# Token attention: raw score products issued ahead of the bilinear ones by half of a unit's heads

## The reference

```python
def _L0_attn_ref(x, ...):                      # H = 16 heads of HD = 8, t = 256 tokens
    qkv = (x @ qkv_w.T).reshape(b, t, 3, H, HD)
    q, k, v = ...                              # each (b, H, t, HD)
    raw = einsum('bhid,bhjd->bhij', q, k)
    scores = sips_alpha * tanh(raw / sips_beta)
    soft_bits = tanh(x @ hex_w.T)              # 6 columns
    scores += lam * einsum('bid,bjd->bij', soft_bits, soft_bits)[:, None] / 2
    hexc = tanh(x @ q6_w.T)                    # 6 columns
    scores += einsum('bid,hde,bje->bhij', hexc, Mh, hexc) / 6 * (2 * sigmoid(scale_logit))
    attn = softmax(where(causal, scores, -inf))
    return (attn @ v) ... @ out_w.T
```

## Time and profile before

| | |
|---|---|
| median of 3 runs | 4148.58 us (4145.99 to 4149.01) |
| profiled execution, its own time | 4149.29 us |
| span of the profiled execution | 4147.5 us, so 1.8 us lie around it |
| token stage, from the start of the span | about 0 to 905 us |
| busy over the span: PE, DVE, ACT, POOL | 94%, 74%, 64%, 45% |
| products of L607 and of L613 | 2048 passes each (1024 of 256 columns, 1024 of 128) |

### The profile page before, as it was taken

The page is one execution under the profiler, slowest core; times in us unless marked ns, Lnnn a source line. Parts: engine busy times, 40 slices in busy tenths (PEclk is TensorE's granted clock), DMA queues, the critical chain, the costliest instruction groups (busy, mean ns, idle before and its releaser), DMA issues. The chain is left out here.

```text
span 4147.5 us, 105164 instructions
## 1 busy us (share of the span) xinstructions
PE 3897.3 (94%) x35227; PEld 3023.3 (73%) x35481; DVE 3050.4 (74%) x7206; ACT 2662.1 (64%) x6345; POOL 1866.7 (45%) x1769
## 2 busy tenths in 40 slices
PE   7999999979999989899999898999999999999999
PEld 6777777756677765577777656777777777789998
DVE  6888888878888875688888685555555565556666
ACT  6888888857777763477777436666666666633333
POOL 4555555547777751466656343333434333321111
PEclk9999999989999999999999999999999999999999
DMA  3000000000000001000000010000000000000000
GB/s 107 1 0 0 0 0 0 0 6 20 19 23 19 23 20 30 14 13 15 13 15 13 22 24 21 1 0 0 0 0 0 0 0 0 0 5 9 9 9 10
DMA packets 68908, 48.04 MB, mean 12 GB/s; under 512 B 38216, under 2 KB 57552, under 8 KB 68688
## 3 DMA queue, kind: packets, MB, share of 16 engines
q1 hardware_dynamic: 68816, 46.82, 4.4%
HBM read 13.01 MB, written 4.19 MB: 4 GB/s over the span
## 5 line engine op out<-in xcount | busy, mean ns | idle before, releaser
L1648 ACT ACTIVATE l_probs<-l_act,l_neg_max 128x128 f32<-128x128 f32 (+1 forms) x1024 | 416.2, 426 | 273.7 <-DVE l_neg_max L1605 271.1
L383 POOL TENSOR_TENSOR t_probs<-t_probs,t_neg_max 128x512 f32<-128x512 f32 x384 | 392.8, 1044 | 392.7 <-DVE t_neg_max L444 392.7
L1585 POOL TENSOR_TENSOR l_probs<-l_probs,l_sums 128x512 f32<-128x512 f32 x384 | 391.6, 1041 | 365.7 <-DVE l_sums L1613 365.7
L1605 DVE TENSOR_REDUCE l_neg_max<-l_act 128x2 f32<-128x512 f32 (+1 forms) x384 | 247.0, 685 | 356.6 <-PE l_act L1760 164.0
L1966 ACT ACTIVATE e_hT<-e_act 128x512 f32<-128x512 f32 x256 | 152.9, 597 | 285.4 <-PE e_act L1987 285.4
L437 DVE SCALAR_TENSOR_TENSOR t_probs<-t_tanh_qk,scalars_sb,t_dve 128x512 f32<-128x512 f32 x384 | 269.6, 744 | 88.4 <-ACT t_tanh_qk L541 39.9
L832 POOL TENSOR_TENSOR w_swappedQ<-w_rawQ,w_table 128x512 f32<-128x512 f32 x128 | 162.3, 1290 | 309.8 <-ACT w_rawQ L1049 309.8
L541 ACT ACTIVATE t_tanh_qk<-t_act,t_inv_beta 128x512 f32<-128x512 f32 x384 | 243.1, 684 | 89.3 <-PE t_act L607 89.0
L1999 PEld LDWEIGHTS e_dve<-e_sb,e_hT 128*128 128x128 f32 x2048 | 268.9, 192 | 13.3
L1085 ACT ACTIVATE w_probs<-w_a,w_bias,w_invQ 128x128 f32<-128x128 f32 x512 | 186.0, 469 | 143.5 <-DVE w_bias L952 143.5
L832 POOL TENSOR_TENSOR w_swappedK<-w_rawK,w_table 128x512 f32<-128x512 f32 x128 | 228.7, 1808 | 92.7 <-ACT w_rawK L1049 92.7
(11 more groups left out here) (259 smaller groups left out, 10672.8 us busy)
## 6 DMA issues: line engine op xcount, KB each, us to landing
w_v_mid<-w_v SPq DMA_DIRECT2D x128, 130.0 KB, 2.3
z<-w_z_copy SPq DMA_DIRECT2D x32, 128.0 KB, 2.0
h<-z SPq DMA_DIRECT2D x32, 128.0 KB
out<-x_sb SPq DMA_DIRECT2D x32, 128.0 KB, 1.8
h<-z SPq DMA_DIRECT2D x32, 127.0 KB
wqkv_sb<-L_ffn_wqkv SPq DMA_DIRECT2D x2, 768.0 KB, 5.9
kv_up_sb<-L_attn_w_kv_up SPq DMA_DIRECT2D x1, 1024.0 KB, 8.4
e_sb<-L_ffn_w SPq DMA_DIRECT2D x1, 1024.0 KB, 5.7
```

The source lines that it names most:

```text
L383: nc.gpsimd.tensor_tensor(p, p, neg_max[:, j, 0:len(gs)].unsqueeze(2) .broadcast_to((P, len(gs), P * (t + 1))), ALU.add).then_inc(shifted. ...
L1585: nc.gpsimd.tensor_tensor(p, p, sums[:, at, 0:len(hs)].unsqueeze(2) .broadcast_to((P, len(hs), P * (t + 1))), ALU.mult).then_inc(divided.s ...
L1605: nc.vector.tensor_reduce(neg_max[:, units.index(name), 0:len(hs)], to_act.bank("s" + name, back)[:, :].rearrange("p (h j) -> p h j", h=le ...
L1648: ins = nc.scalar.activation(probs[:, at % SLOTS, s * width:(s + 1) * width], bank[:, s * width:(s + 1) * width], ACT.Exp, bias=neg_max[:, ...
```

## The change

Only the order in which `scores` issues its products on TensorE changes. The waits for free banks stay ahead of them all; the mask products stay behind them all; operands, shapes, banks, flags and signals of each product stay as they are.

```diff
-                    for s, g in enumerate(gs):
-                        at, tile, last = slice(s * width, (s + 1) * width), slice(P * t, P * t + P), s == len(gs) - 1
+                    tile = slice(P * t, P * t + P)
+
+                    def raw(s, name):
+                        far = rows((unit(name)[0] + GROUPS // 2) % GROUPS)
+                        ins = nc.tensor.matmul(to_act.bank("raw" + name, back)[:, s * width:(s + 1) * width],
+                                               q[u][far, gs[s], tile], k[u][far, gs[s], 0:width],
+                                               start=s == 0, stop=s == len(gs) - 1)
+                        if s == len(gs) - 1:
+                            ins.then_inc(to_act.filled.sem, 1)
+
+                    def bil(s, name):
+                        near = rows(unit(name)[0])
+                        nc.tensor.matmul(to_dve.bank("bil" + name, back)[:, s * width:(s + 1) * width],
+                                         left[u][near, gs[s], tile], bits[u][near, 0:width],
+                                         start=s == 0, stop=False)
+
+                    behind_raw = len(gs) // 2
+                    for s in range(len(gs) + behind_raw):
                         for name in names:
-                            far = rows((unit(name)[0] + GROUPS // 2) % GROUPS)
-                            ins = nc.tensor.matmul(to_act.bank("raw" + name, back)[:, at], q[u][far, g, tile],
-                                                   k[u][far, g, 0:width], start=s == 0, stop=last)
-                            if last:
-                                ins.then_inc(to_act.filled.sem, 1)
-                        for name in names:
-                            near = rows(unit(name)[0])
-                            nc.tensor.matmul(to_dve.bank("bil" + name, back)[:, at], left[u][near, g, tile],
-                                             bits[u][near, 0:width], start=s == 0, stop=False)
+                            if s < len(gs):
+                                raw(s, name)
+                            if s >= behind_raw:
+                                bil(s - behind_raw, name)
```

## The result

The changed kernel takes 4153.5 us (median of 20 runs, 4147.5 to 4155.6) against 4147.1 us (20 runs, 4143.1 to 4149.9): a ratio of **1.0014**, 95% interval 1.0007 to 1.0020. The ratio gives 5.8 us more (2.9 to 8.3), the difference of the medians is 6.4 us. The profiled execution has 4152.8 us (span 4151.0) against 4149.3. In these two traces the start of the last block of scores lies 867.5 us behind that of the first after the change, 863.0 us before: all that the profiled execution lost, 3.5 us, is lost in the token stage.

A forecast was written before the change was run, and what follows sets the result against it. TensorE sets the token stage's pace (748.92 of 800 us busy), VectorE close behind. Later mask products cost 0 to 3.4 us, taken as 2: profiled 4149.3 + 2 = 4151.3, median 0.7 lower, so 4150.6 us, range 4145 to 4156.

The forecast's parts named there:

- the wait that it had named as cover: TensorE's idle time ahead of L607 on VectorE's probabilities copy and combine, 1.1 us per sequence, which could absorb the delay.
- the step that failed: Score blocks: each row group works through its own list from block start, so all passes keep their times; cost nothing.
- Rival 2: Score blocks: limited row-group room makes a and b stand idle; 4200 us, most of it 4163 to 4205, chance 0.27.
- its point: Row-group queue: the stall decides from where more than one product waits; 7 instructions in two-head, 11 in four-head blocks.
- its sign in the timeline: Block start: only L607 passes, L613 beginning 0.2 to 0.45 us later, and TensorE's waits on VectorE partly reduced.
- its case of two products' room: With room for two products per row group, only four-head blocks are hit, 0.22 us each: 14 us, 4163 us.
- Rival 1: Score blocks: raw banks finish earlier by program order, shortening TensorE's loop waits by 12 us; 4137 us, chance 0.09.
- The rule of the Trainium skill that I had weighed: TensorE: matmuls start and end strictly in program order, only weight loads pulled ahead; a block would take 1.94 us.

The follow-up runs named there:

- `left` on 128 rows: Kernel before with products left0 and left1 on 128 rows instead of 12 (zero rows added): -10.0 us, 0.9972; same edit on the changed kernel: +0.4 us, 0.9998.
- one head ahead: Kernel before with raw products running one head ahead of bilinear ones in both kinds of block: +2.1 us, ratio 1.0006.
- pairs: Kernel before with products issued in pairs of one row group (A0 A1 B0 B1 a0 a1 b0 b1) in both kinds of block: -1.5 us, ratio 0.9998.
- longer bilinear lists: Kernel before, old order, each four-head block doing its first bilinear products of each twin three times: +13.8 us, ratio 1.0033.
- All raw first: Kernel before with all raw products of a block issued ahead of all its bilinear ones: +38.3 us, ratio 1.0096.
- three of A first: Kernel before with four-head blocks only reordered to start A0 A1 A2 B0 a0 b0: +6.0 us, ratio 1.0015.
- filled wait: Kernel before with three overwritten 512-column products ahead of turn 4's wait for bilinear banks: -1.0 us, ratio 0.9997.
- the last run: Kernel before with turn 4's raw products issued after the raw-bank wait alone, bilinear ones after their own wait: -4.8 us, ratio 0.9988.

## Why the prediction was right, and where it was not

- **Forecast and bounds.** 4150.6 us, +2 us, in a range of 4145 to 4156; measured 4153.5 us, +5.8 us or 0.14%, inside that range and clear of zero. That it came out so near is luck: the forecast had missed a stall of 20.8 us in all, and most of that was taken away by the wait that it had named as cover and by the clock, for which it had no term.
- **Two-head blocks: right.** Four rounds, four row groups in step, mask 0.014 us later (expected 0.013), no time that can be measured in the run with these blocks alone.
- **Four-head blocks: the step that failed** is "If a row group starts on its list as soon as the block begins, then every pass starts where it does now": the row groups of a and b start 0.33 us late. I priced the four-head block at 0.027 us; it costs 0.325 us. Rival 2 named the mechanism ("a row group can hold only so much"), its point (7 instructions fit, 11 don't) and its sign in the timeline (L613 starting 0.2 to 0.45 us late); its case of two products' room holds. Its size was off: 0.22 us a block instead of 0.325, since A2 is taken in when A0's second pass is over (0.33 us), not when it starts (0.22 us).
- **The sum of that rival, with the measured size,** would have been 0.325 x 64 + 0.015 x 128 = 22.7 us, and too high. Two terms were missing from it. TensorE's wait ahead of turn 1 shrank: with no half-clock stretches about (`left` on 128 rows), the mean distance from turn 0 to turn 1 is 4.01 us without the change and 3.73 with it, 0.28 x 32 = 9 us, seen in the waits on the combine (10.4 and 3.4 us). That is the cover of 1.1 us per sequence that I had named, of which a quarter was used. And eight half-clock stretches fewer: the kernel before has 863.0 - 852.7 = 10.3 us more than with the edit of `left`, for ten stretches, so 1.0 us each, 8 us in all. 22.7 - 9 - 8 = 5.7 us; measured 5.8. The close agreement is luck too: between the two kernels with `left` on 128 rows the same account gives 22.7 - 9 = 13.7 us, and the medians are 10.4 us apart, the two traces' blocks 12.9; and in the changed kernel a step with a stretch is 1.6 us longer and the next no shorter, so that its two cost 3 us and not 2. The account holds to some 3 us.
- **Why fewer stretches.** Shown: they go when the `left` products use all rows, and come in one place of the step. The products on 12 rows are not enough for one: they stand in every step of every kernel without that edit, and most steps have no fall. That the changed kernel has two where the kernel before has ten goes with its undisturbed steps of 27.2 to 27.6 us against 26.8 to 27.2; one head ahead and pairs, in between, have six and five. The granted clock over the span, 0.986 to 0.989 in all 20 runs of the changed kernel and 0.982 to 0.986 in all runs of the kernel before beside the experiments, says the same as the two traces. Why a longer step meets fewer of them was not tested, and longer is not always better. The longer bilinear lists, at 27.5 to 27.7 us, had four. All raw first, with undisturbed steps of 27.75 us, 0.71 x 32 = 23 us more than 27.04, had five stretches of 6.8 us in a row, with steps of 30.8 us there (3.1 us more each), and three of 3.4 us with steps of 29.3 us (1.5 us more). That makes 23 + 15 + 5 - 10 (the ten of the kernel before) = 33 us, which is what the two traces show; the median is 38 us up, the traced execution having been the fastest of its four.
- **Rival 1, raw banks earlier: wrong here.** Behind the same waits no order made the last raw pass of a block start earlier: in a four-head block it stands at 0.89 us in all of them but two, where it is later (0.99 in pairs, 1.21 with three of A first). The rule of the Trainium skill that I had weighed ("TensorE: Matmul & The Clock Gate", "The mechanism": matmuls start strictly in program order) is not what the traces show for passes in different row groups: in the pairs run b0 starts 0.04 us after A0, with A0's second pass and both passes of A1, which stand ahead of it, unstarted.
- **A second rule of that page.** The Trainium skill, "TensorE: Matmul & The Clock Gate", section "Why this matters for your kernels", puts falls of the clock in mid-kernel down to gaps in which TensorE idles. The filled wait does not agree (no gap there, nine falls), nor do the 15 falls of the last run, each with TensorE busy right up to it.

## What to carry to other kernels

Where products use different row groups, their order in the program was free up to a point and worth nothing here, and behind that point it cost: keep the row groups' lists balanced, so that a third fp32 product of a row group does not stand ahead of another group's work while the first is still under way. When a longer block costs less than its length, look at the granted clock and at the next wait before believing that it was covered; here, by the account above, they took 8 and 9 us of 23. Products that use few rows are worth a trial with rows of zeros: here that cost nothing and gave 10 us.

## What the runs showed of the hardware that I had not expected

- A row group of TensorE takes in two fp32 products (8 instructions: two weight loads and two passes each; 7 of them can wait, 11 can't); a third one in the program holds back everything behind it, other row groups too, until the first is done (0.33 us after the block's start for 128 columns, 0.56 us where a fourth has to come in too).
- Products on 12 rows, 2.0 us of them, stood ahead of every fall to 1.2 GHz in the kernel before, between 40 and 890 us; with 116 rows of zeros added no fall was left, while filling the wait of 0.86 us ahead of them changed nothing. Each of its falls lasted 3.4 us and cost 1.0 us of time on average.
